# Rolling 44 of 64 unrolled attention units into two hardware loops per engine

## The chip, the cores and the metric

The kernel runs on one core of one Trainium2 chip. The metric is device microseconds of one launch; less is better. Before the change the median of three runs is 2289.9 us (2286.05 to 2307.46).

## What is computed

A batch of 8 sequences of 512 tokens with 128 features goes through four layers, each with a residual and a layer norm behind it. The first two (a gated selective scan and a top-1 mixture of experts) lie ahead of the change. The last two are attention, and the change lies in them:

```python
x = L0_attn_x
x = _layernorm(x + _L0_attn_ref(x, ...), axis=-1)      # selective scan
x = _layernorm(x + _L0_ffn_ref(x, ...), axis=-1)       # 8 experts, top 1
x = _layernorm(x + _L1_attn_ref(x, w_Q, w_K, w_V), axis=-1)   # 16 heads of 8
x = _layernorm(x + _L1_ffn_ref(x, ...), axis=-1)       # below
# _L1_ffn_ref: six nodes, each an attention of 8 heads of 16 over earlier nodes
for c in range(6):
    q = ew[c, 0] * (nodes[in_q] @ We[eq] + be[eq])
    k = ew[c, 1] * (nodes[in_k] @ We[ek] + be[ek])
    v = ew[c, 2] * (nodes[in_v] @ We[ev] + be[ev])
    nodes[c] = act_w[c] * _mha(q, k, v, Wq[c], Wk[c], Wv[c], Wo[c]) + q
```

## The kernel before

**Units.** All attention work is cut into 64 units of 8 heads over one sequence. Units 0 to 15 are the 16-head layer (two units a sequence; the class `kc`), units 16 to 63 are six nodes times eight sequences (`kn`). A unit has the number u = 4 q + r, with r from 0 to 3 (`RING` = 4 sets of stacked queries and keys) and q from 0 to 15 (`QU` = 16; `QC` = 4 is the first q of the nodes).

**A unit on the engines.** Each unit is two halves k of four heads, and each half is eight steps i, written out by hand in one `body(c, q, r)` for each engine. In a step TensorE (PE) computes two score tiles of a later unit (`scores`, into `bank_s`), of which VectorE (DVE) takes the row maxima (`reduce`), and one pair of transposed score tiles of the present unit (`scoresT`, into the two slots of `bank_x`), of which ScalarE (ACT) takes the exponential (`exp`). In four steps of each half PE also multiplies by the values (`output`, into `bank_o`). Between these stand the projections of units one to three ahead, the transposes and, in the nodes, the output projection. GpSimd (POOL) splits the projected queries and keys into high and low parts (`split`), and SyncE (SP) issues every DMA: the loads of a unit, 12 to 16 copies that stack query and key rows (`stack`), two that put the maxima beside the queries (`rows_m`), and the store of a node.

**What sets the order.** Each engine runs its `body` for q = 0 to 15 and r = 0 to 3, through `units(e, body)`, which is plain Python: all 64 units are written out in each engine's program. Engines meet only at counting semaphores. `need(e, sem, value)` waits until a semaphore has reached a value, which is a number where q is a Python number. An instruction carries one wait; where it needs several, the others stand in instructions of their own ahead of it, and such a wait holds up the engine's issue. `Slots` hands out the two slots of `bank_x` in turn and remembers who read each last; `misc` does the same for `bank_m` in the variable `reader`.

**Loops that are there already.** The first two layers run through `staged(e, body, depth)`: the first and last batches written out, and a hardware loop (`e.Fori`) between, whose counter is a register. These loops are short: at most 39 matmuls or 44 DVE instructions a pass. In them each wait's value is worked out from the counter by register instructions.

The lines that the text names, by the kernel before: PE scores L1038, scoresT L1061, output L1078, maxima L1048, turn L1092, value L1024, projections L990, L1003, L1011; DVE reduce L1475, parts L1486 and L1489, divide L1501 and L1508; ACT exp L827, evacuations L748, L758, L769, L787, L795; SP stack L457, rows_m L442, loads L411 to L425. The change adds eleven lines above them, so that in its program PE's scores are L1049 and ACT's exp L838.

Of the kernel before, what the change touches and what calls it, by code (L numbers as in the profile page):

```python
# [26 lines left out]
RING = 4  # L27
# [24 lines left out]
def build(nc, a):  # L52
# [7 lines left out]
    with ExitStack() as ctx:  # L60
# [146 lines left out]
        S = {}  # L207
# [50 lines left out]
        def at_(c, q, r):  # L258

            x = Kind()  # L260
            x.q, x.r = q + r // RING, r % RING
            x.u = RING * x.q + x.r
            if isinstance(q, int):
                if not 0 <= x.u < U:
                    return None
                c = kc if x.u < UC else kn
            x.c, x.un = c, x.u - UC
            x.b = 2 * x.q + x.r // 2
            x.half = x.r % 2
            x.turn = x.q - QC * c.node  # L270
            return x
# [4 lines left out]

        def units(e, body):

            for q in range(QU):
                for r in range(RING):  # L280
                    body(None, q, r)

        def final(x):

# [28 lines left out]
        def paced(x, node, first):  # L313

            return node if x.c.node else first
# [592 lines left out]
        def _(pe):  # L908
# [5 lines left out]
            def body(b):  # L914
                b0, b1, b2 = b, b - 1, b - 2
                if batch(b0):
                    now(pe, "a_hn", b0)
                    before(pe, "a_hT_ev", b0)
                    for t in range(NT):
                        mm = pe.transpose(bank_m[:, t * P:(t + 1) * P], hn[:, t * P:(t + 1) * P], ident[:, :])  # L920
                    mm.then_inc(S["a_hT_ps"], 1)
                    now(pe, "a_hT_ev", b0)
                    before(pe, "a_xs_ev", b0)
                    before(pe, "a_g_ev", b0)
                    for j in range(2 * NH):
                        mm = pe.matmul(sec(bank_x[:, j // NH, :], j % NH), w_in[:, j * P:(j + 1) * P], hT, start=True, stop=True)
                    mm.then_inc(S["a_win_ps"], 1)
                if batch(b2):

                    now(pe, "a_sp", b2)  # L930
                    before(pe, "a_mb_ev", b2)
                    for k in range(NH):
                        pe.matmul(bank_o[COL:COL + NS, :], mean_w[:, :], rl[:, k, :], start=(k == 0), stop=(k == NH - 1))
                        mm = pe.matmul(bank_o[0:NS, :], bmt[:, k, :], xs_at(b2, k), start=(k == 0), stop=(k == NH - 1))
                    mm.then_inc(S["a_mb_ps"], 1)
                if batch(b1):
                    now(pe, "a_xs", b1)
                    before(pe, "a_z_ev", b1, NH)
                    for h in range(NH):
                        for k in range(NH):  # L940
                            mm = pe.matmul(bank_s[:, h, :], wd[:, k, h * P:(h + 1) * P], xs_at(b1, k),  # L941
                                           start=(k == 0), stop=(k == NH - 1))
                    mm.then_inc(S["a_z_ps"], 1)
# [270 lines left out]
            for n in range(4):  # L1214
                scores(at_(kc, 0, 1), 0, n)

            def body(c, q, r):
                x, last, ahead = at_(c, q, r), at_(c, q, r - 1), at_(c, q, r + 3)
                steps = paced(x, 2, 4)
                for k in range(2):  # L1220
                    for i in range(8):
                        one, two = led(c, q, r, k, i)
                        scores(*one)
                        scoresT(x, k, i)
                        scores(*two)
                        if i == 1:
                            maxima(*led_group(c, q, r, k))
                        output(*((last, 1) if k == 0 else (x, 0)), 1, i, steps)
                        output(x, k, 0, i - 4, steps)
                        if i == paced(x, 3, 5):  # L1230
                            turn(*((last, 1) if k == 0 else (x, 0)))
                        if k == 0:
                            if i == paced(x, 2, 7):
                                value(at_(c, q, r + 1))
                            if i == 6:
                                turn_ctx(last)
                            if i == 7:
                                out_proj(last)
                        else:
                            if i == 1:  # L1240
                                turn_final(last)
                            if i == 2:
                                proj_q(ahead)
                                proj_kh(only(ahead, False))
                            if i == 6:
                                proj_kh(only(ahead, True))
                            if i == 7:
                                proj_qh(ahead)
                                turn_x3(last)
            units(pe, body)  # L1250
            end = at_(kn, QU - 1, RING - 1)
            for step in range(2):
# [405 lines left out]
```

## Time and profile before

| what | value |
|---|---|
| median of 3 runs | 2289.9 us |
| the profiled execution, device time | 2289.9 us |
| its span, first to last instruction | 2288.1 us |
| PE busy | 2074.0 us, 91% |
| DVE busy | 1740.4 us, 76% |
| ACT busy | 1475.9 us, 65% |
| POOL busy | 341.5 us, 15% |
| mean granted PE clock | 0.941 of full speed |

Busy time counts work on the engine, not register, branch, semaphore or DMA-issuing instructions. A PE matmul's end is modelled. "issue" in a view is time in which an engine waited for nothing that the profile shows.

### The profile page before, as it was taken

Reading aid. Unit: us, or ns where it says so; the run is one execution under the profiler, and the core shown is the slowest. Engines: PE = TensorE matmul, PEld = TensorE weight load, DVE = VectorE, ACT = ScalarE, POOL = GpSimd, SP = SyncE. Lnnn points to the kernel's source line nnn. Section 1 sums busy time; section 2 is a strip of 40 time slices with the busy share of each in tenths; the row PEclk is TensorE's granted clock in tenths of the full one; section 3 lists DMA queues with packets and bytes.
Section 4 is the critical chain, followed back from the end, with each engine's and each line's share of the span. In section 5 each row is a group of like instructions: output and inputs, shape, how many; then the busy total and the mean of one; then the engine's idle time right before and its main releaser. Section 6 shows DMA issues by size and latency. Waiting matters only on the chain.

```text
span 2288.1 us, 34387 instructions
## 1 busy us (share of the span) xinstructions
PE 2074.0 (91%) x11820; PEld 863.7 (38%) x11820; DVE 1740.4 (76%) x3501; ACT 1475.9 (65%) x2004; POOL 341.5 (15%) x385
## 2 busy tenths in 40 slices
PE   5748882999999999999999999999999999999995
PEld 2224441343444444334343343333333334443332
DVE  5846982678777777777777777777777777778884
ACT  4734560366666666777777777777777777776664
POOL 1100125000000011111111111111111111113223
PEclk9977885699999999999999999999999999999998
DMA  3001112333323345556555555655556565665630
GB/s 100 18 23 60 43 47 47 50 62 70 71 65 69 79 98 110 103 111 111 105 105 106 105 106 106 105 106 105 106 106 106 109 107 108 108 107 97 102 55 25
DMA packets 137198, 195.68 MB, mean 86 GB/s; under 512 B 20152, under 2 KB 55632, under 8 KB 137040
## 3 DMA queue, kind: packets, MB, share of 16 engines
q1 hardware_dynamic: 137040, 193.63, 43.7%
q8 instruction: 92, 1.51, 0.3%
q14 instruction: 66, 0.54, 0.1%
HBM read 75.45 MB, written 23.73 MB: 43 GB/s over the span
## 4 chain that ended last, share of the span: by engine, by line
PE 70%; DVE 15%; issue 7%; ACT 3%; POOL 2%; SPq 1%; DMA 1%; DVEq 0%; POOLq 0%; ACTq 0%
PE bank_s L1038 23%; PE bank_o L1078 19%; PE bank_x L1061 6%; DVE big L1475 6%; PE bank_m L1092 3%; PE bank_x L1003 3%; PE bank_x L1024 3%; PE bank_x L1011 2%; ACT big L827 2%; PE bank_x L990 2%; PE bank_m L1112 2%; DVE big L1282 2%; PE bank_s L941 1%; DVE big L1521 1%; DVE big L1273 1%
## 5 line engine op out<-in xcount | busy, mean ns | idle before, releaser
L1475 DVE TENSOR_REDUCE big<-bank_s 128x1 f32<-128x512 f32 x2048 | 1337.6, 684 | 378.1 <-PE bank_s L1038 371.6
L827 ACT ACTIVATE big<-bank_x 128x1024 f32<-128x1024 f32 x1024 | 1045.9, 1022 | 452.5 <-PE bank_x L1061 437.2
L1038 PE MATMUL bank_s<-kst,qst 48*128 48x512 f32 x2048 | 848.6, 473 | 38.9 <-DVE big L1475 27.2
L1061 PE MATMUL bank_x<-qst,kst 50*128 50x512 f32 x2048 | 754.8, 449 | 6.1 <-ACT big L827 1.9
L1038 PEld LDWEIGHTS bank_s<-kst,qst 48*128 48x128 f32 x2048 | 356.2, 188 | 712.7 <-DVE big L1475 631.9
L1078 PE MATMUL bank_o<-big,at 128*32 128x512 f32 (+1 forms) x5104 | 582.5, 529 | 3.0 <-ACT big L827 2.0
L1061 PEld LDWEIGHTS bank_x<-qst,kst 50*128 50x128 f32 x2048 | 305.6, 187 | 30.2 <-ACT big L827 22.4
L607 POOL CAST at<-at 128x512 fp32r<-128x512 f32 x112 | 68.1, 608 | 1310.4 <-ACT at L758 1030.4
L1078 PEld LDWEIGHTS bank_o<-big,at 128*32 128x32 f32 x5104 | 102.3, 109 | 174.5 <-issue 155.1
L609 POOL TENSOR_TENSOR at<-at 128x512 fp32r<-128x512 f32 x112 | 143.2, 1279 | 10.4 <-POOL at L607 0.9
L795 ACT ACTIVATE at<-bank_o 128x512 f32<-128x512 f32 x128 | 76.4, 597 | 38.6 <-PE bank_o L1078 38.6
L1282 DVE TENSOR_SCALAR big<-big 128x128 f32<-128x128 f32 x192 | 61.8, 393 | 41.7 <-POOL big L600 40.7
L835 ACT ACTIVATE big<-bank_x,big 128x128 f32<-128x128 f32 x256 | 68.7, 376 | 27.7 <-PE bank_x L1138 19.1
L1092 PE MATMUL bank_m<-ident,at 128*128 128x128 f32 x512 | 85.0, 289 | 1.0 <-ACT at L795 0.7
L598 POOL TENSOR_TENSOR big<-big,eps_ln 128x4 f32<-128x4 f32 x40 | 13.7, 344 | 469.5 <-DVE big L1277 469.5
L1138 PE MATMUL bank_x<-xw,big 128*128 128x512 f32 x128 | 74.7, 726 | 1.0 <-ACT big L835 1.0
L1092 PEld LDWEIGHTS bank_m<-ident,at 128*128 128x128 f32 x512 | 54.2, 141 | 49.6 <-issue 47.3
L1465 DVE TENSOR_REDUCE big<-big 128x128 f32<-128x1024 f32 x32 | 60.9, 1903 | 6.3 <-ACT big L835 6.3
L1011 PE MATMUL bank_x<-at 128*128 128x512 f32 x96 | 52.8, 632 | 3.5
L1112 PE MATMUL bank_m<-big,at 128*128 128x512 f32 x96 | 55.0, 655 | 0.7 <-issue 0.7
L1024 PE MATMUL bank_x<-at 128*128 128x128 f32 x384 | 55.6, 288 | 0.0
L990 PE MATMUL bank_x<-at 128*128 128x512 f32 x96 | 53.9, 643 | 0.7 <-ACT big L819 0.7
(151 smaller groups left out, 1494.9 us busy)
## 6 DMA issues: line engine op xcount, KB each, us to landing
at<-nodes_d SPq DMA_DIRECT2D x144, 256.0 KB, 5.5
kst<-at SPq DMA_DIRECT2D x288, 128.0 KB
qst<-at SPq DMA_DIRECT2D x288, 128.0 KB
nodes_d<-big SPq DMA_DIRECT2D x48, 256.0 KB, 2.9
at<-w_d SPq DMA_DIRECT2D x48, 193.0 KB, 5.7
at<-x2T_d SPq DMA_DIRECT2D x32, 256.0 KB, 4.3
kst<-at SPq DMA_DIRECT2D x128, 64.0 KB
qst<-at SPq DMA_DIRECT2D x128, 64.0 KB
```

The source lines that it names most:

```text
L609: pool.tensor_tensor(dst[:, 1, :], src, dst[:, 0, :], ALU.subtract).then_inc(done, n)
L827: act.activation(PT[:, kp, h, :, :], ring.take()[0].rearrange("p (c n) -> p c n", c=2), ACT.Exp, scale=x.c.scale).then_inc(S["c_ex"], 1)
L990: pe.matmul(to[:, 0:L], t[:, 0:P], t[:, WA:WA + L], start=True, stop=True).then_inc(S["c_qT_ps"], 1)
L1011: pe.matmul(to[:, 0:L], st_qk[x.half][:, P:2 * P], q_sb[x.r], start=True, stop=True).then_inc(S["c_qh_ps"], 1)
L1024: mm = pe.matmul(to[:, k * n:(k + 1) * n], t[:, P + k * P:P + (k + 1) * P], w, start=True, stop=True)
L1038: pe.matmul(bank_s[:, n % 2, :], qst[rows, x.r, h, t * P:(t + 1) * P], kst[rows, x.r, h, :], start=True, stop=True).then_inc(S["c_s_ps"], 1)
L1061: mm = pe.matmul(sec(to, j), kst[rows, x.r, h, kc_ * P:(kc_ + 1) * P], qst[rows, x.r, h, :], start=True, stop=True)
L1078: mm = pe.matmul(bank_o[COL * h:COL * (h + 1), cols], vaug[x.half][:, 2 * kp + j, GH * k + h, :], PT[:, kp, h, j, cols], start=(kp == 0 an ...
L1092: mm = pe.transpose(bank_m[:, t * P:(t + 1) * P], ot_sb[:, t * P:(t + 1) * P], ident[:, :])
L1112: pe.matmul(bank_m[:, :], st_o[x.half][:, 0:P], ctxT, start=True, stop=True).then_inc(S["c_wo_ps"], 1)
L1282: i = dve.tensor_scalar(dst[:, t * D:(t + 1) * D], src[:, t * D:(t + 1) * D], mv_[:, t, 0:1], rs_[:, t:t + 1], ALU.subtract, ALU.mult)
L1475: dve.tensor_reduce(nm[:, k, at_n:at_n + 1], bank_s[:, n % 2, :], AX.X, ALU.max, negate=True).then_inc(S["c_red"], 1)
```

## The change

`units` no longer writes out all 64 units. It writes out q = 0; runs q = 1 and 2 as a hardware loop of two passes; writes out q = 3 and 4; runs q = 5 to 13 as a hardware loop of nine passes; and writes out q = 14 and 15. A pass is four units. All five engines use it, so each has two loops whose counters stand in its own registers. 44 of the 64 units now run in loops. In PE's `body` the readers of the slots are set by formulas of the counter where a pass begins and put back to numbers where it ends.

```diff
         def units(e, body):
 
-            for q in range(QU):
+            for r in range(RING):
+                body(kc, 0, r)
+            with e.Fori(1, QC - 1) as it:
+                for r in range(RING):
+                    body(kc, it, r)
+            for q in (QC - 1, QC):
                 for r in range(RING):
                     body(None, q, r)
+            with e.Fori(QC + 1, QU - 2) as it:
+                for r in range(RING):
+                    body(kn, it, r)
+            for q in (QU - 2, QU - 1):
+                for r in range(RING):
+                    body(kn, q, r)
@@
+            def ring_reader(c, q):
+
+                return S["c_ot_ev"], 2 * RING * q - 1
+
+            def slot_readers(c, q):
+
+                last_ = (S["c_ex"], 16 * RING * q)
+                two = [last_, (S["c_qf_ev"], RING * q + 3 - UC)] if c.node else [(S["c_ex"], 16 * RING * q - 1), last_]
+                return two if ring.n % 2 == 0 else two[::-1]
+
             def body(c, q, r):
                 x, last, ahead = at_(c, q, r), at_(c, q, r - 1), at_(c, q, r + 3)
+                in_loop = not isinstance(q, int)
+                if in_loop and r == 0:
+                    reader[0] = ring_reader(c, q)
+                    ring.readers = slot_readers(c, q)
                 steps = paced(x, 2, 4)
@@
+                if in_loop and r == RING - 1:
+                    reader[0] = ring_reader(c, QU - 2 if c.node else QC - 1)
+                    ring.readers = slot_readers(c, QU - 2 if c.node else QC - 1)
```

The tensor instructions and their order on each engine stay as they were. What changes is what stands between them. On PE, the end of a unit of the nodes and the start of the next read as follows in the program before. In brackets are the semaphores waited for; `c_red` counts DVE's maxima, `c_ex` ACT's exponentials, `c_q_ev`, `c_qf_ev` and `c_kf_ev` ACT's evacuations, `c_m_dma` the copies of the maxima.

```order
L1038 MATMUL bank_s<-kst,qst 128x512 [waits c_red]
L1061 MATMUL bank_x<-qst,kst 128x512 [waits c_ex]
L1061 MATMUL bank_x<-qst,kst 128x512
L1038 MATMUL bank_s<-kst,qst 128x512 [waits c_red]
L1011 MATMUL bank_x<-at 128x512 [waits c_kf_ev,c_q_ev]
L1038 MATMUL bank_s<-kst,qst 128x512 [waits c_red]
L1061 MATMUL bank_x<-qst,kst 128x512 [waits c_ex,c_m_dma]
L1061 MATMUL bank_x<-qst,kst 128x512
L1038 MATMUL bank_s<-kst,qst 128x512 [waits c_red]
```

In the changed program the same place, at the end of a pass of the second loop, is:

```order
L1049 MATMUL bank_s<-kst,qst 128x512 [waits c_red]
L49 REGISTER_ALU
L1072 MATMUL bank_x<-qst,kst 128x512 [waits c_ex]
L1072 MATMUL bank_x<-qst,kst 128x512
L49 REGISTER_ALU
L1049 MATMUL bank_s<-kst,qst 128x512 [waits c_red]
L49 REGISTER_ALU [waits c_q_ev]
L1022 MATMUL bank_x<-at 128x512 [waits c_kf_ev]
L287 REGISTER_ALU
L287 COMPARE_AND_BRANCH
```

and the pass begins, on PE, with:

```order
L287 ISA
L1049 MATMUL bank_s<-kst,qst 128x512 [waits c_red]
L49 ISA
L49 REGISTER_ALU [waits c_m_dma]
L1072 MATMUL bank_x<-qst,kst 128x512 [waits c_ex]
L1072 MATMUL bank_x<-qst,kst 128x512
L49 REGISTER_ALU
L1049 MATMUL bank_s<-kst,qst 128x512 [waits c_red]
```

Nothing moved against anything else; register instructions (REGISTER_ALU, and ISA, which does up to six register operations in one) came in between, and the pass ends with a jump back. By the program's order a pass of the second loop has, beside its matmuls, 196 REGISTER_ALU and 30 ISA on PE; 130 and 15 on DVE; 96 and 32 on ACT; 17 and 48 on SP; 11 and 8 on POOL. A pass of the first loop has 184 and 29 on PE, 129 and 17 on DVE, 87 and 32 on ACT.

On ACT the end of a unit of the nodes was:

```order
L758 ACTIVATE at<-bank_x,at 128x512 [waits c_sp,c_kh_ps]
L827 ACTIVATE big<-bank_x 128x1024 [waits c_st_ps]
L769 ACTIVATE at<-bank_x 128x512 [waits c_sp,c_qh_ps]
L827 ACTIVATE big<-bank_x 128x1024 [waits c_pv_ps,c_st_ps]
L827 ACTIVATE big<-bank_x 128x1024 [waits c_st_ps]
```

and is now, at the end of a pass (`c_st_ps`, `c_kh_ps` and `c_qh_ps` count PE's results, `c_sp` POOL's splits):

```order
L49 REGISTER_ALU
L49 ISA [waits c_kh_ps]
L769 ACTIVATE at<-bank_x,at 128x512 [waits c_sp]
L49 REGISTER_ALU
L838 ACTIVATE big<-bank_x 128x1024 [waits c_st_ps]
L775 ACTIVATE at<-bank_x 128x512 [waits c_sp,c_qh_ps]
L287 REGISTER_ALU
L287 COMPARE_AND_BRANCH
```

Here, too, the tensor work keeps its order. Where an instruction has two waits, the one that stands ahead of it in an instruction of its own (and holds up issue) is now often the other of the two.

## Rows read from the trace of the kernel before

**Rows 1.** The page: span, then busy us (share) and instructions of each engine.
```profile
span 2288.1 us, 34387 instructions
PE 2074.0 (91%) x11820; PEld 863.7 (38%) x11820; DVE 1740.4 (76%) x3501; ACT 1475.9 (65%) x2004; POOL 341.5 (15%) x385
```
**Rows 2.** Busy by window: window, PE, PEld, DVE, ACT, POOL, PEclk, DMA share, GB/s.
```profile
530.00:588.50 58.50, 55.82 (x437) 23.83 (x441) 48.04 (x96) 38.76 (x47) 4.97 (x6) 1.00 0.36 81
...
1516.87:1544.97 28.10, 27.71 (x158) 11.16 (x159) 22.30 (x42) 20.69 (x26) 3.73 (x4) 1.00 0.62 107
...
1509.98:1517.88 7.90, 7.81 (x41) 3.06 (x40) 6.78 (x14) 5.83 (x7) 0.92 (x2) 1.00 0.01 3
```
**Rows 3.** The chain that ended last, pieces of PE's last projection of a unit.
```profile
1488.76 1.10 PE bank_x L1011 x2
1516.87 1.10 PE bank_x L1011 x2
1544.97 1.10 PE bank_x L1011 x2
```
**Rows 4.** DVE in order of time, the expert stage's loop, then the pass written out after it.
```profile
231.26 0.19 DVE L1417 TENSOR_TENSOR big<-big 128x32 f32<-128x32 f32 x1
231.37 0.17 DVE L1419 RECIPROCAL big<-big 128x4 f32<-128x4 f32 x1
231.57 0.19 DVE L1421 TENSOR_TENSOR big<-big 128x32 f32<-128x32 f32 x1
...
330.64 0.19 DVE L1417 TENSOR_TENSOR big<-big 128x32 f32<-128x32 f32 x1
330.75 0.17 DVE L1419 RECIPROCAL big<-big 128x4 f32<-128x4 f32 x1
330.95 0.19 DVE L1421 TENSOR_TENSOR big<-big 128x32 f32<-128x32 f32 x1
```
**Rows 5.** SP's DMA issues in the expert stage's loop: a pass that jumps back, the last pass.
```profile
222.00 0.37 SPq L536 DMA_DIRECT2D x2T_d<-big  x1
223.00 0.41 SPq L514 DMA_DIRECT2D big<-in_x  x1
...
302.05 0.36 SPq L536 DMA_DIRECT2D x2T_d<-big  x1
302.62 0.40 SPq L514 DMA_DIRECT2D big<-in_x  x1
```
**Rows 6.** PE and DVE where the first layer's loop jumps back.
```profile
91.60 3.70 PE L941 MATMUL bank_s<-big,wd 128*128 x8
95.14 0.60 PE L920 MATMUL bank_m<-ident,big 128*128 128x128 f32 x4
95.34 1.41 DVE L1343 TENSOR_SCALAR big<-bank_s,cv 128x512 f32<-128x512 f32 x2 [1.46 <-PE bank_s L941]
96.67 0.99 DVE L1349 TENSOR_SCALAR big<-big,cvh 128x512 f32<-128x512 f32 x2
```
**Rows 7.** The page's DMA queues: packets, MB, share of 16 engines.
```profile
q8 instruction: 92, 1.51, 0.3%
q14 instruction: 66, 0.54, 0.1%
```
**Rows 8.** DMA issues: count, KB each, us from issue to landing.
```profile
bmt<-in_bmt SPq DMA_DIRECT2D x1, 16.0 KB, 3.0
at<-w_d SPq DMA_DIRECT2D x48, 193.0 KB, 5.7
```
**Rows 9.** All engines in order of time around the end of a unit of the nodes.
```profile
1508.11 0.25 ACT L787 ACTIVATE big<-bank_m 32x128 fp32r<-32x128 f32 x1
1509.99 0.66 PE L1092 MATMUL bank_m<-ident,at 128*128 128x128 f32 x4
1516.03 0.69 ACT L758 ACTIVATE at<-bank_x,at 128x512 f32<-128x512 f32 x1
1516.46 1.29 DVE L1475 TENSOR_REDUCE big<-bank_s 128x1 f32<-128x512 f32 x2 [0.27 <-PE bank_s L1038]
1516.87 1.10 PE L1011 MATMUL bank_x<-at 128*128 128x512 f32 x2
1518.72 1.02 ACT L827 ACTIVATE big<-bank_x 128x1024 f32<-128x1024 f32 x1
1521.49 0.49 PE L1061 MATMUL bank_x<-qst,kst 50*128 50x512 f32 x1
```

## The prediction

> **What bounds the kernel now.** I read the page first: over the span of 2288.1 us PE is busy 91%, DVE 76%, ACT 65% [rows 1]. An average hides stages, so I asked for busy time by window. In the nodes a unit lasts 28.10 us and PE is busy for 27.71 of them, at full clock, while DVE has 22.30 and ACT 20.69 [rows 2]. In the 16-head layer two units take 58.50 us, with PE busy for 55.82 [rows 2]. The chain that ended last says the same: the last projection of each unit stands on it, 28.11 and 28.10 us apart [rows 3]. So PE's array is the bound in the part that the change touches, its spare time is 0.4 us a unit in the nodes and 1.3 in the layer before, and DVE and ACT have 5.8 and 7.4 us a unit in reserve. No matmul is removed or added. The change can act in two ways only: through what now stands between the matmuls (register work and other waits), and through the jumps back at the end of passes.
>
> The 44 units that go into loops are 8 of the 16-head layer (8 x 29.25 = 234 us) and 36 of the nodes (36 x 28.10 = 1012 us). A loop of two passes jumps back once, one of nine passes eight times: 9 jumps on each engine.
>
> **Register work.** A pass of four node units gets 226 register instructions on PE (196 and 30), 145 on DVE, 128 on ACT. The price of one I take from SP in a loop that exists. Between two DMA issues at a jump back there are 223.00 - 222.37 = 0.63 us; in the last pass, which falls through, 302.62 - 302.41 = 0.21 us [rows 5]. In the first gap stand a counter addition, a compare and branch, an address instruction and two that the order does not show (a register move and a wait already met): about 0.1 us each, an estimate from these rows. On PE that makes 226 x 0.1 = 23 us of issue in a pass of 112.4 us. It is paid only if issue, not the array, is what PE runs out of. Before, PE issues 441 + 437 = 878 matmuls and weight loads in 58.5 us of the 16-head layer, so one costs it at most 0.067 us, and 158 + 159 = 317 in 28.1 us of the nodes [rows 2]. At that upper price a node pass needs 4 x 317 x 0.067 + 23 = 108 us, still under 112.4. DVE shows directly that register work can vanish: three dependent small instructions start 0.11 and 0.20 us apart in the loop of the expert stage, and 0.11 and 0.20 in the pass written out [rows 4]. I take 0 us. The ends are a gain of 44 x 0.4 = 18 us, if the freed order of waits took away all of PE's spare time, and the loss of the third rival below. What hides it is that issue runs ahead of the array while the array works; where it cannot run ahead, each register instruction ahead of a matmul shows at 0.1 us.
>
> The other of two waits now holds up issue. On PE that helps a little: in front of the transposed scores it is the copies of the maxima, long there, instead of an exponential. On ACT it is often PE's result itself, so ACT can no longer decode ahead. That delays an exponential by perhaps two register instructions, 0.2 us. Its cover is this: the exponential that starts at 1518.72 ends at 1519.74, and the scores that need its slot start at 1521.49, 1.75 us later [rows 9]. I take 0.
>
> **The jump back.** The short loops show what it costs when the code is at hand: nothing. PE starts the next pass at 95.14, before the modelled end of the last matmul (91.60 + 3.70 = 95.30), and DVE goes on at 96.67 with the previous pair ending at 96.75 [rows 6]. But these bodies are short. The page has two queues of kind instruction, 92 packets of 1.51 MB and 66 of 0.54 MB [rows 7]: 2.05 MB for 34387 executed instructions, about 60 bytes for each. Code is fetched by DMA while the kernel runs, in pieces of 16.4 KB on the larger queue. A node pass on PE is 4 x 317 + 226 = 1494 instructions, about 90 KB by that rate, six pieces. If the first piece of a body is gone when its end is reached, each jump waits for a fetch. No row shows such a wait. The nearest is a DMA of the same size, 16 KB in 3.0 us; the load of 193 KB in the loaded phase takes 5.7; at the other end stands 0, the short loops [rows 8]. I take 3.0 us and 0.4 for the jump itself (0.63 - 0.21): 3.4 us in which an engine issues nothing.
>
> The Trainium skill (Advanced Engine Details and Errata, ISA Cache) says that an engine holds 32 KB of instructions, TensorE 128 KB, in only two lines; the size of the pieces agrees with the 16 KB line it gives, and by it DVE's body of over 256 instructions does not stay. By that rule the fetch comes at every jump; it would make the 3.4 us certain rather than likely, and leaves the sum as it is.
>
> What of the 3.4 us reaches the array depends on how far issue is ahead when it meets the jump.
>
> PE: the last wait that holds issue up is for ACT's copy of the maxima, over at 1508.36, for a transpose that the array begins at 1509.99: issue is at most 1.6 us ahead there [rows 9]. From there to the end of the unit the array has 7.90 us of work, 41 matmuls and 40 loads [rows 2], and by the changed program 20 register instructions stand between. At 0.067 us for each of the 81, issue needs 5.4 + 2.0 = 7.4 us and is 1.6 + 0.5 = 2.1 us ahead at the jump; at half that price it would be 4.8. Only the 0.067 rests on a row, so I take a value near it: 2.5 us of cover, and 3.4 - 2.5 = 0.9 us lost at each jump.
>
> ACT: issue is held until PE's projection of the keys is there, about 1516.03; the next pass's first exponential starts at 1518.72, and PE needs its slot 1.75 us after it ends: 2.7 + 1.75 = 4.4 us of cover [rows 9], over 3.4. Nothing lost.
>
> DVE: its last two maxima of the unit run from 1516.46 [rows 9] and their waits do not hold up issue. If it issues several instructions ahead its cover is some 4 us; if only one, about 1.3. I take 0 lost, since PE's own loss comes at the same place and covers it. SP and POOL have waits of many us in each unit, so a late pass there reaches nobody.
>
> The skill's table of queue depths (the same page, Engine Queue Depths) gives TensorE 64 entries, ScalarE and VectorE 8. By 64 entries PE could be 64 x 28.1 / 317 = 5.7 us ahead, an estimate, and would lose nothing; that is the first rival's case. No row shows the depth.
>
> **The sum.** 9 jumps x 0.9 us = 8 us. The profiled execution took 2289.9 us, its span 2288.1 and 1.8 around it, and it is at the median of the runs. 2289.9 + 8 = 2298 us.
>
> **Rivals.**
>
> *All is hidden.* Issue on PE is 3.4 us or more ahead at the jump, or the bodies stay at hand. For it: the steadiness of 28.10 us through code that is fetched all the way [rows 3, 7], and the short loops. Against: bodies of some 90 KB. Time: 2289.9 plus at most one register instruction a jump, 2290 to 2292 us.
>
> *The jump is bare.* The fetch takes 3.4 to 5.7 us and little of it is covered, because a fetch is late on DVE or ACT as well as on PE and the array waits for whichever is last. The place is the first step of passes 2 to 9 of the second loop (and pass 2 of the first). For it: the DMA engines are 62% busy there [rows 2], so a fetch queues. 9 x 3.4 = 31 to 9 x 5.7 = 51 us: 2321 to 2341 us, slower. It decides from a loss of 2.6 us a jump on (23 us, 1%).
>
> *Issue becomes the bound.* If a matmul or load does cost PE 0.067 us, a pass of the 16-head loop needs 4 x 439 x 0.067 + 213 x 0.1 = 139 us instead of 117, 44 us over two passes: 2342 us with the jumps. For it: that is where PE issues most per us. Against: 0.067 is only an upper bound, and there PE also waits for others. PE would show idle "issue" throughout the loop and not at its head.
>
> *Faster.* Changed waits give back PE's spare time: at most 18 us, 2272 us. Against: that idle time is DVE's and ACT's cadence, not issue.
>
> **How the numbers follow.** Chances: forecast 0.35, all hidden 0.32, bare jump 0.21, issue bound 0.08, faster 0.04. About 1%, or 23 us, is what a measurement of this kernel can tell from no change. Above 2313 us lie the bare jump, most of the issue rival and a tenth of the forecast, whose cover may be smaller: 0.31. Below 2267 us lies next to nothing: 0.02. The rest, 0.67, is within 1%. The range runs from 2286 us, just under the hidden case, to 2332 us, the middle of the bare jump; outside it lie about 0.04 below and 0.12 to 0.15 above.
>
> **What would show it.** Right: units within a pass still 28.1 us apart, and 29 us across a jump, with PE idle by "issue" at the first scores or transposed scores of the pass; about 2 MB on the instruction queues as before, since each pass fetches its code anew. If the megabytes fall to the share of code that is new (by the order less than 60%), the bodies stay and the first rival holds. Wrong: units in the middle of a pass longer than 28.1 us (issue is the bound, or register waits cost more than their cover), jumps of 31 us and more (bare jump), or DVE or ACT, not PE, as the engine that comes late at a jump. A time under 2280 would say that I misread what PE's spare time is.

## The result, and the profile after

The changed kernel takes 2368.12 us (median of 4 runs, 2357.50 to 2372.26); the kernel before, on the same chip, 2293.82. The ratio is 1.031 with a 95% interval of 1.025 to 1.037: slower. I had forecast 2298 us, 2286 to 2332. The profiled execution took 2356.44 us, 66.5 more than the one of before (2289.9). Ratios here are of runs in the fast state alone; of the kernels below only that of experiment 2 had others, two of ten, which its median counts in.

The page of the changed kernel: span, busy time by engine, the granted clock in 40 slices, and the two instruction queues (packets, MB), which answer to [rows 1, 7].

```profile
span 2354.4 us, 40695 instructions
...
PE 2116.2 (90%) x11820; PEld 879.7 (37%) x11820; DVE 1742.3 (74%) x3501; ACT 1476.5 (63%) x2004; POOL 341.3 (14%) x385
...
PEclk9967885678998999999899999899999899999998
...
q8 instruction: 54, 0.88, 0.2%
q14 instruction: 79, 0.65, 0.1%
```

PE does the same 11820 matmuls, yet is busy 42 us longer; DVE and ACT are not. The clock row has dents at regular distances. TensorE's instruction queue, q8, has shrunk from 92 packets to 54. That of the other engines, q14, has grown from 66 to 79 although their program is shorter. Experiments 1 to 3 show which queue is whose.

The chain that ended last (start, us, step) places the loss. L1022 is the last projection of a unit, L1011 in [rows 3]:

```profile
1108.99 1.13 PE bank_x L1022 x2
...
1137.97 2.19 issue
...
1141.56 1.96 issue
...
1174.90 1.13 PE bank_x L1022 x2
...
1202.97 1.12 PE bank_x L1022 x2
```

Inside a pass units are 28.04 to 28.11 us apart, 28.07 in the mean (as from 1174.90 to 1202.97), a hair under the 28.10 of before. Behind the one at 1108.99 the next starts at 1137.08, and from there to 1174.90 it is 37.82 us: that is a jump back. The eight jumps of the node loop take 37.82, 32.81, 32.80, 36.74, 33.81, 34.67, 37.23 and 33.35 us, together 54.7 us over 8 x 28.07. The first unit of the nodes starts at 850.82 us, where it was 837.52: 13.3 us later. 54.7 + 13.3, less 36 x 0.03 for the units inside, is 66.9, within 0.4 of the whole difference.

Not all of the 13.3 us belongs to the first loop's jump. The last score tile ahead of that jump starts at 664.33 us; the same tile started at 658.57 before. These 5.8 us lie ahead of any jump of the two new loops, and in eight traces (experiment 3) that tile starts anywhere from 655.1 to 664.3, whether loops are rolled or not. From that tile to the nodes it reads, before and after (us, PE, PEld, DVE, ACT, POOL, PEclk, DMA share, GB/s):

```profile
658.57:837.52 178.95, 171.31 (x1295) 72.07 (x1296) 141.13 (x282) 114.23 (x137) 13.36 (x17) 0.95 0.33 72
```

```profile
664.33:850.82 186.49, 175.97 (x1295) 74.98 (x1296) 141.38 (x282) 114.13 (x137) 13.34 (x17) 0.92 0.32 69
```

So the first loop's jump costs 7.5 us: PE is idle for 2.9 us more, and busy for 4.7 us more with the same 1295 matmuls, at a lower mean clock.

Who is late at a jump, by the changed kernel's waits (sum us, count, longest):

```profile
DVE big L1503 <- issue: 35.0, 16, 2.7
```

The kernel before has no such row. 16 is two for each of eight jumps, and here are both in order of time (start, us, engine, line; in brackets the idle time before and what ended it):

```profile
1136.68 1.29 DVE L1503 TENSOR_REDUCE big<-bank_s 128x1 f32<-128x512 f32 x2 [0.27 <-PE bank_s L1049]
...
1140.30 0.69 DVE L1503 TENSOR_REDUCE big<-bank_s 128x1 f32<-128x512 f32 x1 [2.33 <-issue]
...
1141.05 0.50 PE L1049 MATMUL bank_s<-kst,qst 48*128 48x512 f32 x1 [1.18 <-DVE big L1503]
...
1143.52 1.29 DVE L1503 TENSOR_REDUCE big<-bank_s 128x1 f32<-128x512 f32 x2 [2.53 <-issue]
...
1144.27 0.79 PE L1049 MATMUL bank_s<-kst,qst 48*128 48x512 f32 x1 [2.41 <-DVE big L1503]
```

DVE waits 2.33 us for nothing but its own instructions, does one reduction, and waits 2.53 us again. PE needs the score bank that the reduction frees, and stands. Its matmul then takes 0.79 us in place of 0.50. The windows (PE, PEld, DVE, ACT, POOL, PEclk, DMA share, GB/s) say why:

```profile
1137.00:1141.00 4.00, 2.78 (x14) 0.76 (x14) 1.66 (x3) 2.67 (x4) 3.65 (x4) 1.00 0.09 30
1141.00:1144.00 3.00, 0.81 (x3) 0.38 (x3) 0.48 (x1) 1.02 (x1) 0.05 (x1) 1.00 0.96 149
1144.00:1147.00 3.00, 2.73 (x10) 0.58 (x10) 1.50 (x3) 0.00 (x0) 0.00 (x0) 0.50 0.69 82
...
1153.00:1156.00 3.00, 3.00 (x14) 0.69 (x14) 1.62 (x3) 1.02 (x1) 0.00 (x0) 0.50 1.11 128
1156.00:1159.00 3.00, 3.00 (x18) 0.75 (x17) 1.63 (x3) 1.13 (x2) 0.00 (x0) 0.73 1.04 229
1159.00:1162.00 3.00, 2.93 (x12) 1.28 (x12) 2.40 (x6) 2.43 (x3) 0.00 (x0) 1.00 0.39 133
```

After two waits of 1.18 and 2.41 us close together the granted clock drops from 1.00 to 0.50 (2.4 to 1.2 GHz), and stays down for some 13 us in which PE is busy all the time. At the next jump, one of the cheaper ones (32.81 us), it is down for one window of 3 us only:

```profile
1264.00:1267.00 3.00, 1.64 (x10) 0.43 (x10) 1.97 (x3) 0.77 (x1) 0.00 (x0) 0.98 1.02 143
1267.00:1270.00 3.00, 3.00 (x16) 2.28 (x12) 1.29 (x2) 1.77 (x3) 0.00 (x0) 0.50 0.32 40
1270.00:1273.00 3.00, 3.00 (x20) 1.44 (x21) 2.24 (x5) 2.17 (x3) 0.00 (x0) 0.96 0.64 132
```

That is what separates the jumps of 37 us from those of 33. What decides how long it stays down is not shown: PE's waits are 0.97 and 1.66 us at the jump above, and again 0.97 and 1.66 us at the fourth (36.74 us), where the clock is down for some 13 us. A stretch of 36 units, first in the kernel before:

```profile
1056.00:2074.00 1018.00, 1003.52 (x5723) 404.48 (x5720) 807.10 (x1484) 750.02 (x907) 134.03 (x144) 1.00 0.59 108
```

and in the changed one:

```profile
1075.40:2147.40 1072.00, 1032.49 (x5719) 412.92 (x5719) 809.65 (x1495) 749.48 (x904) 137.13 (x148) 0.97 0.56 101
```

The stretch is 54 us longer. PE is busy for 29 us of these, with the same matmuls (5723 and 5719), part of them at half clock, and idle for 25. So more than half of the loss in the node loop is clock, not waiting.

The first loop's single jump looks different. Here PE itself has nothing to issue, and the others wait for it:

```profile
668.55 0.49 PE L1049 MATMUL bank_s<-kst,qst 48*128 48x512 f32 x1 [3.15 <-issue]
669.08 1.29 DVE L1503 TENSOR_REDUCE big<-bank_s 128x1 f32<-128x512 f32 x2 [3.52 <-PE bank_s L1049]
...
669.64 1.02 ACT L838 ACTIVATE big<-bank_x 128x1024 f32<-128x1024 f32 x1 [4.31 <-PE bank_x L1072]
```

### The profile page after: what moved, and what is told of

It reads as the page before. It is cut to its first block, busy times and chain, and to the rows that moved or that the text cites. A ratio compares the mean times of both kernels' runs of the same rounds, so it can differ in the third digit from the quotient of the medians.

```text
span 2354.4 us, 40695 instructions
## 1 busy us (share of the span) xinstructions
PE 2116.2 (90%) x11820; PEld 879.7 (37%) x11820; DVE 1742.3 (74%) x3501; ACT 1476.5 (63%) x2004; POOL 341.3 (14%) x385
## 4 chain that ended last, share of the span: by engine, by line
PE 69%; DVE 15%; issue 8%; ACT 4%; POOL 2%; DMA 1%; DVEq 1%; SPq 0%; POOLq 0%; ACTq 0%
PE bank_s L1049 23%; PE bank_o L1089 19%; DVE big L1503 6%; PE bank_x L1072 5%; PE bank_m L1103 3%; PE bank_x L1035 3%; PE bank_x L1014 3%; ACT big L838 2%; PE bank_x L1001 2%; PE bank_m L1123 2%; PE bank_x L1022 2%; DVE big L1310 2%; PE bank_s L952 1%; DVE big L1301 1%; DVE big L1549 1%
## 5 line engine op out<-in xcount | busy, mean ns | idle before, releaser
L1049 PE MATMUL bank_s<-kst,qst 48*128 48x512 f32 x2048 | 864.4, 482 | 66.0 <-DVE big L1503 52.3
L1072 PE MATMUL bank_x<-qst,kst 50*128 50x512 f32 x2048 | 771.8, 458 | 5.1 <-ACT big L838 1.9
L1049 PEld LDWEIGHTS bank_s<-kst,qst 48*128 48x128 f32 x2048 | 365.4, 192 | 752.5 <-DVE big L1503 693.0
L1089 PE MATMUL bank_o<-big,at 128*32 128x512 f32 (+1 forms) x5104 | 598.6, 542 | 3.4 <-ACT big L838 2.0
L1072 PEld LDWEIGHTS bank_x<-qst,kst 50*128 50x128 f32 x2048 | 312.4, 191 | 29.2 <-ACT big L838 22.4
L1035 PE MATMUL bank_x<-at 128*128 128x128 f32 x384 | 60.4, 304 | 0.0
L1035 PEld LDWEIGHTS bank_x<-at 128*128 128x128 f32 x384 | 50.8, 206 | 19.8 <-issue 19.8
L1022 PE MATMUL bank_x<-at 128*128 128x512 f32 x96 | 53.9, 643 | 3.2
```

The lines of the kernel that those rows point to most:

```text
L1022: pe.matmul(to[:, 0:L], st_qk[x.half][:, P:2 * P], q_sb[x.r], start=True, stop=True).then_inc(S["c_qh_ps"], 1)
L1035: mm = pe.matmul(to[:, k * n:(k + 1) * n], t[:, P + k * P:P + (k + 1) * P], w, start=True, stop=True)
L1049: pe.matmul(bank_s[:, n % 2, :], qst[rows, x.r, h, t * P:(t + 1) * P], kst[rows, x.r, h, :], start=True, stop=True).then_inc(S["c_s_ps"], 1)
L1072: mm = pe.matmul(sec(to, j), kst[rows, x.r, h, kc_ * P:(kc_ + 1) * P], qst[rows, x.r, h, :], start=True, stop=True)
L1089: mm = pe.matmul(bank_o[COL * h:COL * (h + 1), cols], vaug[x.half][:, 2 * kp + j, GH * k + h, :], PT[:, kp, h, j, cols], start=(kp == 0 an ...
```

## The experiments

All times are compared with the kernel before on the same chip. "Node units" are intervals between the last projections of units, as above.

### 1. Only DVE runs loops

```diff
         def units(e, body):
+            if e is not nc.vector:
+                for q in range(QU):
+                    for r in range(RING):
+                        body(None, q, r)
+                return
```

> Only DVE's program is rolled into the two loops; PE, ACT, SP and POOL are written out as before. Theory (DVE fetches the head of the body at each jump, and then a second piece that begins two or three instructions behind the head): the eight jumps of the node loop cost what they cost in the changed kernel, 4.7 to 9.7 us each and some 54 us together, and PE's own stall of 3.2 us at the jump of the first loop is gone: 2340 to 2360 us, ratio 1.020 to 1.030. Rival (PE's fetch, or the register work of all engines together, is what costs, and DVE's idle time only shows it): under 2320 us, ratio under 1.012.

Measured: 2353.23 us, ratio 1.0265 (1.0204 to 1.0325). The eight jumps take 34.62, 34.87, 37.56, 33.67, 34.55, 34.83, 37.52 and 33.68 us; the node units start at 834.0 us, not late. Its waits:

```profile
DVE big L1508 <- issue: 37.9, 16, 2.6
```

```profile
q14 instruction: 95, 0.78, 0.1%
```

DVE's loop alone makes nearly the whole loss, and with all other engines written out. q14 has 29 packets more than the 66 of the kernel before. The late start of the nodes is not DVE's.

### 2. Every engine but DVE runs loops

The condition of experiment 1 turned round (`if e is nc.vector`).

> The opposite: PE, ACT, SP and POOL in loops, DVE written out. Theory: node units are 28.1 us apart across jumps as well, and only the first loop's jump (PE, some 4 us) remains: 2293 to 2305 us, ratio 1.000 to 1.005. Rival (PE's own fetch, or ACT's, is as late and was hidden behind DVE's): 2 to 4 us remain at each of eight jumps, 2315 to 2335 us.

Measured: 2304.69 us, ratio 1.0022 (0.9989 to 1.0055). All units of the node loop are 28.05 to 28.12 us apart, across jumps too. PE's 226 register instructions a pass and ACT's 128 cost nothing, and neither does their jump. In the first loop PE still waits once on issue, for 2.8 us.

```profile
q14 instruction: 50, 0.41, 0.1%
```

The changed kernel, with DVE rolled beside them, has 79 packets on q14: again 29 more, so all that q14 gains is DVE's.

### 3. Only PE runs loops

The same condition as in experiment 1, with `nc.tensor`.

> Only TensorE runs the two loops, the other engines have every unit written out as before. Theory (TensorE's body of the first loop does not stay and stalls it once by some 3 us; its node body of 6 pieces stays): TensorE's queue 54 packets and the others' 66, no cost at any node jump (28.1 us), an idle of about 3 us on issue at the first loop's jump, node units start 8 to 14 us later than in the kernel before (845 to 852 us), 2296 to 2309 us. Rival (the late start comes from another engine's loop, ScalarE's or a queue's): node units start at 834 to 840 us, 2288 to 2298 us.

Measured: 2298.99 us, ratio 1.0008 (0.9957 to 1.0059); node units 28.03 to 28.07 us, starting at 843.6. Its PE wait and its queues:

```profile
PE bank_s L1054 <- issue: 3.4, 1, 3.4
```

```profile
q8 instruction: 54, 0.88, 0.2%
q14 instruction: 66, 0.54, 0.1%
```

The nodes start at 834.0, 835.2 and 837.5 us in the three traces in which PE's first loop is written out, and between 843.6 and 850.8 in the five in which it is rolled and nothing else is added to that stretch. PE's stall is there in each of them. Counted from the last score tile ahead of the jump, so that the scatter of what lies ahead is left out, the way to the nodes takes 178.4 to 179.0 us in the three and 186.5 to 189.6 in the five: the jump costs 7.5 to 11 us. PE is idle for 9.4 to 11.1 us of it in place of 6.3 to 7.6; the rest of the difference is busy time, with the mean clock at 0.89 to 0.92 in place of 0.94 to 0.95. That the median of all runs changes by so little in the end (0.1% and 0.2%, with one in both intervals) means that this part is at the edge of what whole runs resolve.

### 4. Eight instructions more on DVE

Is it the length of DVE's body, 322 instructions, or where it lies? Eight increments of a semaphore at the start of DVE's program move all that follows.

```diff
             dve.wait_ge(s_w, 16 * N_W)
             dve.wait_ge(s_c, 7 + NE)
+            for _ in range(8):
+                dve.sem_inc(passed, 1)
```

> The changed kernel with eight semaphore increments more at the start of DVE's program, where DVE waits for weights anyway; they move all of DVE's code by eight instructions, and so where its loop heads lie in the pieces that are fetched. Theory (the second stall of about 2.2 us comes from a piece that begins just behind the head): one stall a jump instead of two, PE idle too briefly for its clock to fall, 8 x 2.5 = 20 us for the node jumps and 5 to 12 in the first loop: 2315 to 2335 us, ratio 1.010 to 1.018. Rival (both stalls belong to any jump, the branch and the loop's register setup): no change, 2355 to 2372 us.

The eight make DVE's program only seven instructions longer (5706 executed, not 5699).

Measured: 2308.96 us, ratio 1.0052 (1.0017 to 1.0088). Better than I expected: not one stall of two is gone, both are, at every jump. From the chain, over the first jump of the node loop (1133.07 to 1161.15):

```profile
1133.07 1.12 PE bank_x L1022 x2
1161.15 1.13 PE bank_x L1022 x2
```

```profile
q14 instruction: 39, 0.32, 0.1%
```

The body is as long as before, q8 stays at 54 packets, and q14 falls from 79 packets to 39: 40 packets, five for each of eight jumps, were code fetched again. Length alone does not decide.

### 5. Passes of eight units, three jumps

```diff
-            with e.Fori(QC + 1, QU - 2) as it:
-                for r in range(RING):
-                    body(kn, it, r)
+            with e.Fori(0, 4) as it:
+                for s_ in range(2):
+                    for r in range(RING):
+                        body(kn, it * 2 + (QC + 1 + s_), r)
...
```

At the dots stands the rest of the edit: the end that is written out begins one q earlier, at QU - 3, and the readers that PE's body puts back at the end of a pass are those of QU - 3.

> The node loop has passes of eight units: four passes and three jumps instead of nine and eight, with the last of the nine quads written out; first loop as in the change. As many register instructions a unit. Theory (cost by the jump, 6.8 us on average): 3 x 6.8 = 20 us there and 5 to 12 us in the first loop: 2317 to 2335 us, ratio 1.010 to 1.018. Rival (cost by the register work in the body): 32 of 36 units still pay, 2350 to 2365 us.

Measured: 2321.98 us, ratio 1.0129 (1.0073 to 1.0185). The three jumps take 34.13, 33.02 and 34.51 us, the other units of the loop 28.07. The loss goes with the number of jumps. Both queues grow:

```profile
q8 instruction: 107, 1.75, 0.4%
q14 instruction: 102, 0.84, 0.2%
```

PE's body is twice as long now and is fetched again as well, 14 pieces at each jump, and yet a jump costs no more than where DVE alone fetched again. Here it is PE itself that is late. Its branches back (number, shortest, median and longest in ns; the shortest is the last, which does not jump):

```profile
L287 PEldq COMPARE_BRANCH  x4: 83/3718/3865, 1243.8 to 1934.9; - x4
```

The same branch takes at most 0.22 us where PE's body stays (experiment 4). So this run shows the cost to go with the jumps, but its cause at a jump is not the same as in the changed kernel.

### 6. The first loop written out, DVE's node body 53 instructions further on

```diff
-            with e.Fori(1, QC - 1) as it:
-                for r in range(RING):
-                    body(kc, it, r)
-            for q in (QC - 1, QC):
+            for q in range(1, QC + 1):
```

> The changed kernel with its first loop (the 16-head units) written out again for every engine; only the node loop stays rolled. Theory (placement): what is missing at a jump depends on how many fetched blocks of 256 instructions the body touches. Here VectorE's node body (322 instructions) starts 53 static instructions further on than in the changed kernel, so it touches two blocks and not three: the eight node jumps cost nothing (units 28.1 us apart also there, where the changed kernel shows 33 to 38), and the node units start as early as before, since TensorE's first-loop body is written out (node phase from 834 to 840 us, not 851). Time 2288 to 2300 us. Rival (size alone: a VectorE body above 256 instructions always stalls at its jump): 33 to 38 us at each jump, 2330 to 2352 us.

Measured: 2293.63 us, ratio 1.0005 (0.9971 to 1.0038). Node units 28.04 to 28.12 us, jumps included; they start at 835.2.

```profile
q8 instruction: 51, 0.84, 0.2%
q14 instruction: 40, 0.33, 0.1%
```

So the node loop, at most of the code that the change saves, can be had for nothing. It saves no time either.

### 7. 180 and 224 instructions more on DVE

```diff
+            for _ in range(180):
+                dve.sem_inc(passed, 1)
             for n in range(16):
                 reduce(at_(kc, 0, 0), 0, n)
```

> The changed kernel with 180 extra semaphore increments on VectorE, put ahead of its first reduce, where it idles some 20 us. Theory (placement, two blocks of 256 stay): the node body then starts about 177 instructions into a block, 177 + 322 = 499 still ends in the second block, so node jumps stay at 28.1 us; but VectorE's first-loop body (345) now starts about 205 into a block and ends in a third one, so that loop's one jump gets a VectorE stall that it did not have. 2303 to 2318 us (about that of the run with 8 extra instructions, plus 0 to 8 for the first loop). Rival (the extra 8 helped by something other than placement, as timing at the start): nothing says where this one lies; any cost at the node jumps speaks for it.

> The same with 224 extra increments in place of 180. Theory (what counts is whether the body touches three blocks): it starts about 221 into a block, 221 + 322 = 543 passes 512, so at every node jump something is missing again: intervals of 31 to 38 us at the eight jumps, about 40 us on top, 2340 to 2372 us. Rival (only a head that lies within a few instructions of a block's end stalls, since the next block then is wanted at once): this head lies 35 instructions ahead of the end, so jumps cost at most one short stall or nothing, 2303 to 2325 us.

Measured with 180: 2302.42 us, ratio 1.0029 (0.9999 to 1.0060). Node jumps 28.05 to 28.09 us, as the theory wanted, and q14 has 46 packets: 41 for the code and five fetched again, at the first loop's jump. With 224: 2327.58 us, ratio 1.0145 (1.0088 to 1.0203), below the theory's 2340 to 2372:

```profile
q14 instruction: 86, 0.70, 0.1%
```

That is 41 + 45: five packets again at each of nine jumps, as the theory wanted. But the node jumps cost little: 29.45 to 29.53 us at six, 31.3 at two. There the rival was nearer: only one stall is left. At the two dear ones, behind a single wait of PE of 1.21 and 1.22 us, the clock falls all the same:

```profile
1157.00:1160.00 3.00, 3.00 (x16) 1.34 (x11) 1.59 (x3) 1.95 (x4) 0.00 (x0) 0.60 1.08 132
```

The rest of this run's loss lies behind the first loop's jump: 206 us to the nodes, against 186.5 to 189.6 in experiment 3, at a mean clock of 0.78; why the clock is down for so long there is not shown. DVE's own waits, where 20.4 us of the sum is one wait, for the added instructions:

```profile
DVE big L1503 <- issue: 37.9, 9, 20.4
```

Five packets for one jump did not fit my theory of two blocks of 256 instructions, which would be four packets or six. They fit a body that touches four pieces of 128, and one piece more.

### 8. 160 instructions more on PE

The eight on DVE stay, and PE gets 160, ahead of its first value product.

```diff
+            for _ in range(160):
+                pe.sem_inc(passed, 1)
             pe.wait_ge(S["c_ones"], 5 * RING)
```

> The run with 8 extra VectorE increments, and 160 extra increments on TensorE ahead of its first value product, where it idles 34 us. Theory (the same rule with 8 pieces for TensorE: its first-loop body of 1949 instructions, 7.6 pieces, touches nine): if the unseen base of TensorE's code is as VectorE's (about 188), the body now starts about 39 into a piece and ends in the eighth, so that nothing is fetched again: TensorE's queue moves 47 packets, not 54, TensorE's idle of about 3 us on issue at the first loop's jump goes, and the node units start 5 to 11 us earlier than in the run without this pad (837 to 843 us in place of 848). Time 2294 to 2303 us, level with the kernel before. Rival (TensorE's stall is not one of placement): 54 packets, 848 us, 2305 to 2311 us.

Measured: 2326.64 us, ratio 1.0142 (1.0099 to 1.0184). A miss on both counts. The addition was not hidden: PE stood for 23.7 us on it, up to 403.5 us, so that the time says nothing of the first loop. And q8 did not shrink:

```profile
q8 instruction: 56, 0.92, 0.2%
```

Of these, two are more than the 54 of experiment 4. The pieces of PE's queue hold 256 instructions; its program has 45.8 pieces, 46.4 with the addition. So nine pieces are fetched again in the one case and ten in the other, and the starts of the packets behind the jump say the same: nine from 660.2 to 779.9 us in experiment 4, ten from 685.8 to 803.9 us here.

### 9. 128 and 80 instructions more on DVE

The same edit as in 7, to tell pieces of 128 from blocks of 256.

> The changed kernel with 128 extra semaphore increments on VectorE ahead of its first reduce. Theory A (VectorE's code is kept in four pieces of 128 instructions, of which one is the piece fetched ahead, so that a body stays only if it touches three): 128 instructions move the body by exactly one piece, so all stays as in the changed kernel: the head some 3 instructions before a piece's end, two stalls per jump, 5 pieces fetched again at each of eight jumps (VectorE's and the others' queue 80 packets), intervals of 33 to 38 us at the node jumps, 2345 to 2375 us. Theory B (two blocks of 256 stay, as held until now): the body starts 125 into a block, 125 + 322 = 447 ends in the second: nothing fetched again, 40 packets, jumps at 28.1 us, 2296 to 2310 us.

> The same with 80 extra increments. Theory A (pieces of 128, a body of 322 must touch three): it starts 77 into a piece, 77 + 322 = 399 passes 384, so it touches four and 5 pieces are fetched again at each jump, the first loop's (345 instructions) among them: about 85 packets; but the head lies 51 instructions ahead of its piece's end, so only the head's piece is waited for: one stall of 2 to 2.5 us on VectorE at each jump, intervals of 29.4 to 31.5 us at the node jumps, 2310 to 2332 us. Theory B (two blocks of 256): 40 packets, no node jump costs anything, 2296 to 2310 us.

Measured with 128: 2367.35 us, ratio 1.0306 (1.0253 to 1.0358), like the changed kernel itself, with jumps of 36.97, 33.85, 34.74, 37.29, 35.44, 33.40, 37.07 and 33.82 us. Its queue and its waits:

```profile
q14 instruction: 80, 0.66, 0.1%
```

```profile
DVE big L1503 <- issue: 35.4, 16, 2.6
```

With 80: 2316.56 us, ratio 1.0092 (1.0036 to 1.0148), and 85 packets, the number that was forecast:

```profile
q14 instruction: 85, 0.70, 0.1%
```

```profile
DVE big L1503 <- issue: 17.2, 8, 2.4
```

One stall for each jump instead of two. In order of time and by windows its first node jump reads:

```profile
1153.69 2.58 DVE L1503 TENSOR_REDUCE big<-bank_s 128x1 f32<-128x512 f32 x4 [2.12 <-issue]
...
1154.43 0.50 PE L1049 MATMUL bank_s<-kst,qst 48*128 48x512 f32 x1 [0.97 <-DVE big L1503]
```

```profile
1153.00:1156.00 3.00, 2.03 (x17) 0.81 (x13) 2.31 (x4) 1.34 (x2) 1.57 (x2) 1.00 0.49 118
1156.00:1159.00 3.00, 3.00 (x24) 1.66 (x16) 1.59 (x4) 2.34 (x5) 0.00 (x0) 1.00 1.10 131
```

The clock stays at 1.00 here and at the other seven jumps (at one of them behind a wait of PE of 1.25 us), and the jump costs 1.4 us. Theory A held in both runs, B in neither.

### All DVE placements together

The packets of q14 are 8.2 KB each, and 128 more instructions make one packet more (79 and 80): a piece is 128 instructions. Suppose that DVE keeps four pieces, one of them the one fetched ahead. Then a body stays if it touches three: one of 322 instructions if it starts at most 384 - 322 = 62 into a piece, the first loop's (345) at most 39. If the changed kernel's node body starts 125 into a piece, all runs follow. Where it starts is worked out from the packet counts and not shown by a row; only 121 to 127 fits all of them. The first loop's body lies 740 instructions earlier. "8 more" counts as seven (experiment 4).

| DVE code | node body starts at | first loop's at | again, by this rule | q14: code + again | mean cost of a node jump |
|---|---|---|---|---|---|
| changed kernel | 125 | 25 | 8 jumps x 5 | 39 + 40 | 6.8 us |
| 8 more | 4 | 32 | 0 | 39 + 0 | 0 |
| first loop written out | 50 | none | 0 | 40 + 0 | 0 |
| 180 more | 49 | 77 | 1 x 5 | 41 + 5 | 0 |
| 224 more | 93 | 121 | 9 x 5 | 41 + 45 | 1.9 us |
| 128 more | 125 | 25 | 8 x 5 | 40 + 40 | 7.3 us |
| 80 more | 77 | 105 | 9 x 5 | 40 + 45 | 1.5 us |

The trace keeps the start of each packet, and these show the rule at work. In the changed kernel's second node pass, behind the branch at 1137.2 us, q14's start at 1138.2, 1141.0, 1146.7, 1193.8 and 1240.0 us, and the next pass begins with one at 1260.2: every pass has five. DVE goes on at 1140.30 and 1143.52, each time 2.1 to 2.5 us behind the start of a packet. With 80 more the pass's first two start at 1151.8 and 1154.7, and DVE, back at 1153.69, does not stop again. With 8 more q14 has no packet at all from 1130 to 1500 us.

The rule also orders the price. Starting 125 into a piece, the first piece has three instructions left, and the second missing piece is wanted at once: two stalls. Starting at 77 or 93 there are 51 or 35 instructions, which at 112.3 us for 322 last some 18 and 12 us, and the next piece comes in unseen.

For PE the same rule with pieces of 256 and eight kept gives the rest. Its first loop's body has 1949 instructions, 7.6 pieces, and so touches eight or nine; with the one ahead that is nine or ten, never eight, and by this rule no placement helps. Nine and ten are what experiments 4 and 8 show. The node body has 1522. In experiment 4 q8 has six packets in the loop's first pass (1026.2 to 1122.4 us), so that the body touches seven pieces, which with the one ahead makes eight; at the jumps q8 has none up to 2041.6 us.

The Trainium skill (Advanced Engine Details and Errata, ISA Cache) gives 32 KB, in two lines of 16 KB or 256 instructions, and 128 KB on TensorE. The runs agree with both totals: 4 x 8.2 KB and 8 x 16.4 KB. They differ in the size of the piece on VectorE, which is 128 instructions, and they show that one of the pieces is taken up by what is fetched ahead.

## Why the prediction was wrong

**Register work, 0 us: right.** Units inside a pass are 28.04 to 28.11 us apart in the changed kernel, and experiment 2 has that on every engine but DVE.

**Nine jumps are the only cost: right.** The node loop loses at its jumps and nowhere else, and three jumps lose less (experiment 5). The 5.8 us ahead of the first jump are within what this stretch differs by from trace to trace.

**"If the first piece of a body is gone when its end is reached, each jump waits for a fetch": the wrong picture, and the root of the error.** I priced one fetch for each jump, on whatever engine. What decides is how many pieces a body touches against how many are kept. PE's node body and ACT's stay: q8 fell to 54 packets, and q14 to 39 where DVE's stays too (experiment 4). DVE's goes as a whole, and since it starts at the very end of a piece, it waits twice. I had read the Trainium skill's rule (Advanced Engine Details and Errata, ISA Cache) as one of size, that DVE's body of over 256 instructions does not stay, and so as the same for any placement; eight instructions more refute this (experiment 4). Nor did I see that [rows 7] has two sizes of piece: 0.54 MB in 66 packets is 8.2 KB each.

**PE's loss of 0.9 us a jump (3.4 less 2.5 of cover): wrong term.** In the nodes PE has none. In the first loop it has one stall of 2.6 to 3.7 us on issue in all traces in which that loop is rolled on PE, after its cover. The 3.4 us for the fetch and the jump were about right. PE's branch there, which lasts until the next pass begins, takes 3.85 us in the changed kernel (the longest of two; 3.4 to 4.4 in the other traces):

```profile
L281 PEldq COMPARE_BRANCH  x2: 83/1965/3847, 664.5 to 788.0; - x2
```

On DVE it is 3.1 us from the branch at 1137.2 to the next pass's first maximum at 1140.30, of which 2.33 show.

**DVE: "I take 0 lost, since PE's own loss comes at the same place and covers it": this is the step that failed most.** I had two values of DVE's cover, some 4 us and about 1.3, and took the good one without a row that spoke for it. In the changed kernel the cover is 3.1 less 2.33, or 0.8 us: one maximum. With a single stall the wait is 2.12 us although DVE had been busy to 1151.57, and the jump costs 1.4 us (experiment 9): the small cover was nearer, and still too large. I should also have asked who waits for DVE there. PE does, at every score tile, for the bank that the maximum frees.

**The clock was not in the sum.** A loss was counted as the time in which PE stands. With two stalls some 3 us apart at each jump, PE idles about 25 us over the eight jumps and works 29 us more at the lower clock. A single stall left the clock at 1.00 at fourteen of sixteen jumps (experiments 7 and 9) and brought it down for 3 us at two. This, and not the second wait alone, makes a jump cost 4.7 to 9.7 us with two stalls, against 1.4 with one (3.2 where the clock fell).

**"About 2 MB on the instruction queues as before": wrong, and so was the test I tied to it.** I wrote that fewer megabytes would speak for the first rival. They fell to 1.53 MB, since PE's loop stays, while DVE's refetch hides in the smaller queue. The right test is each queue apart against its own code.

**The rivals.** The bare jump had the place and the engine ("a fetch is late on DVE"), but its 3.4 to 5.7 us a jump ended at 2341. Measured are 6.8 a jump in the nodes, for two fetches in a row and the clock, and 7.5 in the first loop (up to 11 in other traces), where PE is the late engine. *All is hidden* describes PE and ACT in the nodes, and the node loop alone as it is in experiment 6 (2293.63 us). Issue as the bound and the gain show nowhere.

Open: when a wait brings the clock down and for how long. PE waits of 1.21 and 1.22 us did and one of 1.25 us did not, and the same two waits cost 3 us of low clock at one jump and 13 at another. TensorE's rule was only counted in packets; no run made its first loop's body fit. No run beat the kernel before; the nearest, experiment 6, is level with it.

## What to carry to other kernels

Before a long body is rolled, count each engine's instructions in pieces and add the piece fetched ahead: on these runs DVE keeps a body that touches three pieces of 128, PE one that touches seven of 256. If it nearly fits, a few dummy instructions ahead of the loop can take its refetch away; the sign to look for is an instruction queue with more packets than the program has pieces. Price a stall by who waits behind it and by the clock: two short stalls in a row cost 6.8 to 7.3 us a jump here, and one 1.5 to 1.9.

## What the runs showed of the hardware

- Eight instructions on one engine moved the time by 2.6% (2368 to 2309 us).
- A stall for one missing piece shows as 1.7 to 2.7 us on DVE behind what cover it has, and as 2.6 to 3.7 us on PE. Without cover it is 3.1 us on DVE and 3.4 to 4.4 us on PE.
- PE's granted clock went to 0.50 after waits of 1.18 and 2.41 us with 0.5 us of work between, and came back some 13 us later although PE was busy all that time; at the next jump it was back after 3 to 4 us. After single waits of 0.95 to 1.02 us (13 jumps) it did not fall, after 1.21 and 1.22 us it did for 3 us, and after one of 1.25 us it did not.
- Fetching 14 pieces of PE's code anew at each jump (experiment 5; 4.9 to 6.4 us a jump) cost no more than DVE's refetch by itself (experiment 1; 5.6 to 9.5).
